# V transposed by VectorE and by a round trip through DRAM instead of by TensorE, in a convolutional attention block

## The reference, cut to what matters

```python
xn = group_norm(x)                       # x: (128, 384, 14, 14), 32 groups
q  = bn(conv1x1(xn, qw))                 # 8 heads x 32,   196 tokens
k  = bn(conv1x1(xn, kw))
v4 = bn(conv1x1(xn, vw))                 # 1024 channels = 8 heads x 128
vl = bn(depthwise_conv3x3(v4))
attn = q @ k.T * 32**-0.5 + bias         # (8, 196, 196) for each image
attn = mix_heads(attn, th1)
attn = softmax(attn)
attn = mix_heads(attn, th2)
o = relu(attn @ v + vl)
out = x + bn(conv1x1(o, pw))
```

## Time and profile before

| what | value |
|---|---|
| time, median of 3 | 4813.96 us (4813.76 to 4814.5) |
| the profiled execution, its own time | 4811.84 us |
| its span, first to last instruction | 4810.0 us |
| TensorE busy | 4779.1 us, 99% |
| VectorE busy | 4175.9 us, 87% |
| ScalarE busy | 3251.4 us, 68% |
| GpSimd busy | 988.6 us, 21% |
| DMA queue 1 | 119.93 MB, 7.4% of 16 engines |
| mean granted TensorE clock | 0.998 |
| one pair in the steady state | 74.50 us |

### The profile page before, as it was taken

One profiled execution on the slowest core, in us unless ns is written; L12 is line 12 of the kernel. 1 busy time (PEld: TensorE's weight loads), 2 busy tenths in 40 slices (PEclk: granted clock), 3 DMA queues, 4 the chain that ended last, 5 costly groups with the idle time before them and its releaser, 6 DMA issues.

```text
span 4810.0 us, 111468 instructions
## 1 busy us (share of the span) xinstructions
PE 4779.1 (99%) x35842; PEld 4760.2 (99%) x35842; DVE 4175.9 (87%) x10897; ACT 3251.4 (68%) x8005; POOL 988.6 (21%) x1093
## 2 busy tenths in 40 slices
PE   7999999999999999999999999999999999999999
PEld 7999999999999999999999999999999999999999
DVE  8888888889888898888888988889888888898887
ACT  6666666666667666667666666766666766666665
POOL 3212212121121221221212212122121221221211
PEclk9999999999999999999999999999999999999999
DMA  1000000000000000000000000000000000000000
GB/s 57 26 20 30 19 26 30 15 30 25 20 30 15 30 25 20 30 15 30 30 15 30 25 20 30 15 30 25 20 30 15 30 29 16 30 21 24 30 15 26
DMA packets 55148, 120.23 MB, mean 25 GB/s; under 512 B 3650, under 2 KB 5842, under 8 KB 55124
## 3 DMA queue, kind: packets, MB, share of 16 engines
q1 hardware_dynamic: 55124, 119.93, 7.4%
HBM read 81.38 MB, written 38.54 MB: 25 GB/s over the span
## 4 chain that ended last, share of the span: by engine, by line
PE 98%; DVE 1%; issue 0%; DMA 0%; ACT 0%; SPq 0%; DVEq 0%
PE psA L250 43%; PE psA L399 14%; PE psL L250 12%; PE psM L250 10%; PE psM L377 8%; PE psL L377 6%; PE psM L367 2%; PE psL L367 2%; DVE psC L620 1%; PE psA L268 0%; PE psA L263 0%; DMA qa<-in_wqkv 0%; DVE probs L675 0%; DVE x_lo L601 0%; DVE q_lo L650 0%
## 5 line engine op out<-in xcount | busy, mean ns | idle before, releaser
L620 DVE SCALAR_TENSOR_TENSOR psC<-vpad,par,psC 128x406 f32<-128x406 f32 x3072 | 1808.7, 637 | 0.0
L498 ACT ACTIVATE probs<-probs,nmax 112x196 f32<-112x196 f32 x1792 | 799.0, 449 | 649.0 <-DVE nmax L675 641.8
L250 PE MATMUL psA<-x_hi,w_lo 128*128 128x392 f32 x2304 | 795.0, 345 | 8.5 <-DVE x_lo L601 8.5
L250 PE MATMUL psA<-x_lo,w_hi 128*128 128x392 f32 x2304 | 788.9, 342 | 0.0
L250 PE MATMUL psA<-x_hi,w_hi 128*128 128x392 f32 x2304 | 788.1, 342 | 0.0
L399 PE MATMUL psA<-qa,shared 105*128 105x196 f32 x4096 | 693.9, 330 | 3.0 <-DVE shared L719 3.0
L399 PEld LDWEIGHTS psA<-qa,shared 105*128 105x128 f32 x4096 | 680.2, 191 | 3.3 <-DVE shared L719 3.3
L650 DVE SCALAR_TENSOR_TENSOR q_lo<-q,th,q_hi 128x392 fp32r<-128x392 f32 x1024 | 604.4, 621 | 34.6 <-ACT q_hi L442 27.6
L719 DVE TENSOR_TENSOR shared<-psA,shared 128x392 f32<-128x392 f32 x512 | 290.1, 567 | 366.5 <-PE psA L399 366.5
L442 ACT ACTIVATE q_hi<-q,th 128x392 fp32r<-128x392 f32 x1024 | 582.0, 620 | 6.0
L434 ACT ACTIVATE o_hi<-shared 128x392 fp32r<-128x392 f32 x512 | 271.5, 530 | 457.6 <-DVE shared L719 457.6
(11 more groups left out here) (85 smaller groups left out, 10500.0 us busy)
## 6 DMA issues: line engine op xcount, KB each, us to landing
xs<-in_x SPq DMA_DIRECT2D x64, 588.0 KB, 3.8
shared<-in_x SPq DMA_DIRECT2D x64, 588.0 KB, 3.8
out<-shared SPq DMA_DIRECT2D x63, 588.0 KB, 3.0
qa<-in_wqkv SPq DMA_DIRECT2D x3, 768.0 KB, 6.7
stage_wp<-in_wp SPq DMA_DIRECT2D x1, 1536.0 KB, 9.9
out<-shared SPq DMA_DIRECT2D x3, 196.0 KB, 2.0
shared<-in_abx SPq DMA_DIRECT2D x1, 165.4 KB
par<-in_par SPq DMA_DIRECT2D x1, 70.5 KB
```

The source lines that it names most:

```text
L250: last = nc.tensor.matmul(dst, w, r, start=(begin and n == 0), stop=(end and n == 2))
L498: nc.scalar.activation(row, row, ACT.Exp, bias=nmax[:, img, b:b + 1], scale=-1.0, accum_out=rowsum[:, img, b:b + 1]).then_inc(s_exp, 1)
L620: nc.vector.scalar_tensor_tensor(a if tap == 7 else sums, src, taps[:, c, TAPS[tap]:TAPS[tap] + 1], a if tap == 0 else sums, MUL, ADD).the ...
```

## The change

TensorE's transposes of V, their eight uses of the banks and the identity matrix go. In their place:

- VectorE transposes V in blocks of 32x32, in two instructions (`turn`), four channel tiles of both images each, 4 x 2 x 7 blocks, so 1,792 elements on each of 128 partitions. The result goes into `turned`, a part of the tensor that will later hold the probabilities. `turn(0)` stands after the first six convolutions, `turn(1)` after three more turns of one `mixed_low` and one convolution; the last five `mixed_low` now come together, and the six convolutions after them.
- SyncE writes the blocks to a DRAM tensor `by_key` with the pixel as its row (`turned_out`, eight DMAs: two images, four groups of 32 partitions, each DMA 32 x 7 pieces of 1 KB), restores a row of ones in the probabilities (`ones_in`), and once all logits of the pair are made reads by_key back with pixels on partitions (`keys_in`, four DMAs of 112 rows of 4 KB, into `raw`, which lies over parts of qa and of q, k_hi and k).
- ScalarE copies from `raw` to `vt`, 105x1024 elements four times (`head_major`), after mixing uses 1, 3, 10 and 13, since the channels arrive ordered by group of 32 first and channel tile second.
- VectorE waits before the scores of use 5 until the eight writes are complete, since the scores overwrite `turned`. TensorE waits for the ones before the mixing.
- k_hi and k_lo are placed so that q, k_hi and k lie next to each other.

```diff
@@ SyncE
+            def turned_out(t):
+                sp.wait_ge(s_turned, 2 * t + 2)
+                for img in range(2):
+                    for a in range(QUADS):
+                        sp.dma_start(by_key[img].rearrange("(b r) (a n) -> r a b n", r=BLK, a=QUADS)[:, a, :, :],
+                                     turned[a * BLK:(a + 1) * BLK, img, :, :, :].rearrange("p b c n -> p b (c n)")
+                                     ).then_inc(s_vt_out, 16)
+            def ones_in(t):
+                sp.wait_ge(s_vt_out, OUTS * (t + 1))
+                sp.dma_start(probs[HP:HP + 1, :, :, :].rearrange("p i b n -> p (i b n)")[:, TURNED_AT:],
+                             A["ones"]).then_inc(s_ones_in, 16)
+            def keys_in(t):
+                sp.wait_ge(s_logit_mm, 14 * (t + 1))
+                for img in range(2):
+                    for jc in range(2):
+                        sp.dma_start(raw[img][0:ROWS, jc, :],
+                                     by_key[img, jc * HALF:jc * HALF + ROWS, :]).then_inc(s_raw[img], 16)
             def step(t, first, last):
                 ...
                     load_x(t + 1)
+                turned_out(t)
+                ones_in(t)
+                keys_in(t)
                 if not first:
                     store(t)
                 residual(t + 1)
@@ TensorE
-                for use in range(22):
-                    img, (what, n) = use // 11, USES[use % 11]
-                    bank_free(use)
-                    if what == "vt":
-                        jc, cg = divmod(n, 2)
-                        for c in range(4):
-                            at_ = PITCH + 1 + img * PITCH * PITCH + jc * HALF
-                            mm = nc.tensor.transpose(mix_bank(use)[:, c * P:(c + 1) * P],
-                                                     vpad[:, 4 * cg + c, at_:at_ + HALF], ident[:, :])
-                        mm.then_inc(s_vt_mm, 1)
+                pe.wait_ge(s_ones_in, 16 * (t + 1))
+                for use, (img, n) in enumerate(USES):      # USES: 2 images x 7
                     if use < 4:
                         pe.wait_ge(s_score, 28 * t + 22 + 2 * use)
                     else:
+                        pe.wait_ge(s_mix_sb, 14 * t + use - 3)
                     ...
                 for img in range(2):
-                    pe.wait_ge(s_vt_sb, 8 * t + 4 * img + 4)
+                    pe.wait_ge(s_vt_sb, 4 * t + 2 * img + 2)
@@ ScalarE
+            def head_major(t, img, jc):
+                act.wait_ge(s_raw[img], 32 * (t + 1))
+                nc.scalar.copy(vt[0:HALF, img, jc, :].rearrange("p (c a n) -> p c a n", c=VT, a=QUADS),
+                               raw[img][0:HALF, jc, :].rearrange("p (a c n) -> p c a n", a=QUADS, c=VT)
+                               ).then_inc(s_vt_sb, 1)
+                COPIES = {1: (0, 0), 3: (0, 1), 10: (1, 0), 13: (1, 1)}
+                for use, (img, n) in enumerate(USES):
+                    act.wait_ge(s_mix_mm, 14 * t + use + 1)
+                    if use == 7:
+                        act.wait_ge(s_vt_sb, 4 * t + 2)
+                    ...  (copy of the bank to attn)
+                    if use in COPIES:
+                        head_major(t, *COPIES[use])
+                    if use == 6 and not last:
+                        act.wait_ge(s_v_mm, VT * (t + 1))
+                        x_high(t + 1)
@@ VectorE
+                def turn(half):
+                    c0 = half * (VT // 2)
+                    dve.wait_ge(s_v_sb, VT * t + c0 + VT // 2)
+                    src = vpad[:, c0:c0 + VT // 2, PITCH + 1:PITCH + 1 + 2 * PITCH * PITCH].rearrange(
+                        "p c (i n) -> p c i n", i=2)[:, :, :, 0:BLOCKS * BLK]
+                    nc.vector.transpose(turned[:, :, :, c0:c0 + VT // 2, :].rearrange("p i b c n -> p c (i b) n"),
+                                        src).then_inc(s_turned, 1)
                 mixed_low(8)
                 convs(6)
-                for _ in range(8):
+                turn(0)
+                for _ in range(3):
                     mixed_low(1)
                     convs(1)
-                convs(1)
+                turn(1)
+                mixed_low(5)
+                convs(6)
                 ...
                 for n in range(RES):
+                    if n == TURNED_ROW // 2:       # 5
+                        dve.wait_ge(s_vt_out, OUTS * (t + 1))
                     wait_alone(dve, s_logit_mm, 14 * t + n + 1)
```

More of the change, by code:

```diff
@@ L19 @@
 HALF = RES // 2 * PITCH
+ROWS = 112
+BLK = 32
+BLOCKS = 7
+QUADS = P // BLK
+PART = VT * BLK
+TURNED = 2 * BLOCKS * PART
+TURNED_AT = 2 * RES * 2 * HALF - TURNED
+TURNED_ROW = TURNED_AT // (2 * HALF)
 HR = P // KD
@@ L173, in mixed @@
                     q[:, kt, :].rearrange("p (b i) -> p b i", i=RES))
-        USES = [("vt", 0), ("mix", 0), ("vt", 1), ("mix", 1), ("vt", 2), ("mix", 2), ("vt", 3), ("mix", 3),
-                ("mix", 4), ("mix", 5), ("mix", 6)]
+        USES = [(img, n) for img in range(2) for n in range(7)]
         def logit_bank(n):
@@ new lines, in step @@
+                    else:
+                        pe.wait_ge(s_mix_sb, 14 * t + use - 3)
+                    pe.wait_ge(s_exp, 28 * t + 14 * img + 2 * n + 2)
+                    pe.wait_ge(s_mixw, 8 * t + 4 * img + group(2 * n + 1) + 1)
+                    bank = mix_bank(use)[:, 0:4 * HP].rearrange("p (j g b i) -> p j g b i", j=2, g=NH, b=2)
+                    for jc in range(2):
+                        for b in range(2):
+                            mm = nc.tensor.matmul(bank[:, jc, :, b, :],
+                                                  probs[0:HP + 1, img, 2 * n + b, jc * HALF:(jc + 1) * HALF],
+                                                  mixw[0:HP + 1, img, 2 * n + b, :].rearrange("p (g i) -> p g i", g=NH),
+                                                  start=True, stop=True)
@@ L382, in step @@
+                    mm.then_inc(s_mix_mm, 1)
                 if first:
@@ L502, in step @@
                         conv_centre(t, CENTRES[n])
[L503 to L514, removed]
-                        nc.scalar.copy(attn[:, img, :, :, 2 * n * RES:(2 * n + 2) * RES], src).then_inc(s_mix_sb, 1)
-                    if use == 16 and not last:
+                COPIES = {1: (0, 0), 3: (0, 1), 10: (1, 0), 13: (1, 1)}
+                for use, (img, n) in enumerate(USES):
+                    act.wait_ge(s_mix_mm, 14 * t + use + 1)
+                    if use == 0 and not first:
+                        act.wait_ge(s_av_mm, 8 * t)
+                    if use == 7:
+                        act.wait_ge(s_vt_sb, 4 * t + 2)
+                    src = mix_bank(use)[:, 0:4 * HP].rearrange("p (j g m) -> p j g m", j=2, g=NH)
+                    nc.scalar.copy(attn[:, img, :, :, 2 * n * RES:(2 * n + 2) * RES], src).then_inc(s_mix_sb, 1)
+                    if use in COPIES:
+                        head_major(t, *COPIES[use])
+                    if use == 6 and not last:
                         act.wait_ge(s_v_mm, VT * (t + 1))
@@ L657, in step @@
                 convs(6)
-                for _ in range(8):
+                if not first:
+                    dve.wait_ge(s_mix_mm, 14 * t)
+                turn(0)
+                for _ in range(3):
                     mixed_low(1)
                     convs(1)
-                convs(1)
+                turn(1)
+                mixed_low(5)
+                convs(6)
                 if not first:
```

46 lines of the change are left out of this document (16 added, 30 removed).

## The result

The changed kernel takes 4881.93 us (median of 4 runs, 4881.75 to 4884.25), the kernel before 4813.9 us beside it: a ratio of 1.0142, 95% interval 1.0126 to 1.0158. I forecast 4841 us. The direction is right and the time lies in the stated range, but the loss is 68 us where I had 27. The profiled execution has a span of 4880.2 us.

The account below looks back on a forecast made before the run. VectorE was to become the bound at 74.4 us a pair, just under TensorE's old 74.50: 4813.96 - 2.5 + 30 us for clock falls = 4841.5, say 4841 us, 0.56% slower; range 4804 to 4940.

Parts of the forecast that it names:

- TensorE's saving: Mixing stage: eight uses of V transposes go, 3.5 us a pair, so the stage falls from 14.26 to 10.7 us.
- T: Start of VectorE's first addition of the AV products in a pair; the logits were forecast at T + 36.6.
- The transposes: VectorE: two added transposes of 128x1792 elements, 1.93 us each, 3.85 us a pair.
- VectorE as the bound, using up 3.29 us of slack: VectorE's chain: the added transposes use up its idle time before the first addition, giving pairs of 74.4 us.
- the recurring 2.46 us: VectorE's wait before the pair's first convolution, for a chain starting after the additions; said to return however late VectorE is.
- ScalarE and the transfers: V's DRAM writes and reads hidden, image 0's reads landing in 4.7 us; head_major copies 1.0 us each, just covered.
- The stall: TensorE stands still 2.4 us a pair before logits use 4, waiting for the scores of use 0.
- six pairs in ten, at 0.8 us, 0.48 us a pair: Clock falls to 1.2 GHz after TensorE's stop: assumed frequency and net price, 30 us over 63 pairs.
- the 1.3 us that I counted: TensorE's spare time per pair against VectorE's chain, said to cover 1.3 us of a clock fall's cost.
- my 0.6 to 2.0 us: Forecast net cost of a clock fall in a pair that has one.
- the time without falls: Whole program with the clock staying up: 2.5 us less, about 4811 us; as a rival, no change, chance 0.25.
- The first pair: VectorE has no slack there already, so the transposes' 3.85 us were added in full.

Follow-up runs that it names:

- fill24: Changed kernel plus 24 harmless 120-column matmuls filling TensorE's stop after logits use 2; 4802.22 us, 0.9976 of the kernel before.
- split_proj: Changed kernel with half of the third projection tile (12 matmuls) moved from behind the logits into the stop after logits use 2; 4803.3 us, 0.9979.
- defer3: Changed kernel with 3 of the 8 convolutions before the second projection's addition moved behind the scores; 4862.35 us, 1.0101.
- tiny_turn: Changed kernel with each VectorE transpose cut to a single 32x32 block, all transfers and ScalarE copies kept; 4654.24 us, 0.9670.
- sums3: Changed kernel with the group sums asked for after logits use 3 instead of use 2, cutting the stop in two; 4853.06 us, 1.0083.
- add_turn: Kernel before, plus VectorE's two transposes and their wait for the mixing, TensorE keeping its own transposes of V; 5110.62 us, 1.0617.
- pool4b: Changed kernel with 4 low parts of scaled queries on GpSimd, only 784 ones loaded behind the logits, ahead of V's reads; 4717.76 us, 0.9800.
- defer7: Changed kernel with 7 of the 8 convolutions before the second projection's addition moved behind the scores; 5151.01 us, 1.0702.
- pool4: Changed kernel with 4 low parts of scaled queries on GpSimd and the whole row of ones loaded behind the logits; 5152.46 us, 1.0701.
- pool6: Changed kernel with 6 low parts of scaled queries on GpSimd and the whole row of ones loaded behind the logits; 5068.19 us, 1.0529.

## Why the loss was two and a half times the forecast

**TensorE's saving: right.** The mixing runs from 2426.75 to 2437.48, 10.73 us (10.7 forecast), the logits begin at T + 36.7 (36.6), and the pair that TensorE alone sets is 71.2 us (71.0).

**The transposes: right.** 1.96 us each (1.93). The Trainium skill, "Vector Engine (DVE) Microarchitecture Reference" (The reshape front-end), by which the estimate was 1.87 us plus start-up, agrees with this row.

**VectorE as the bound, using up 3.29 us of slack: right.** Forecast 74.4 us without falls of the clock; fill24, split_proj and the better pairs of defer3 give 74.22 to 74.24. The first convolution stands 20.46 us behind the first addition (20.4 worked out), the recurring 2.46 us stayed. Without falls the change would have gained 12 us (fill24), where I had 2.5.

**ScalarE and the transfers: right.** head_major took 1.05 us (1.0), image 0's keys landed in 4.2 us (4.7), and tiny_turn shows the whole trip hidden.

**The stall: right size, wrong owner.** 2.68 us where I had 2.4. I followed the bank of psL from use 4 to the scores and overlooked the bank of psA: the group sums wait for the projection's evacuation, which VectorE reaches just before the scores. sums3 shows that the wait I named is next in line, 0.81 us.

**The term that failed: "six pairs in ten, at 0.8 us, 0.48 us a pair".** Both of its factors were too small. The runs show 62 pairs of 62, at 75.33 - 74.22 = 1.1 us in the ordinary pair and 2.6 us in every eighth: 1.29 us a pair, 80 us in all where I had 30. A fall in every pair at my 0.8 us would be 50 us; the other 30 are its price. The fall itself costs 1.7 us of TensorE (defer3, add_turn), of which the spare time behind the logits covers 0.6 us, not the 1.3 us that I counted: VectorE is held up already within the scores (waits up to 0.38 us for late logits in the ordinary pair and none in fill24; from the first convolution to the next addition 54.9 us instead of 53.8), and what VectorE loses there is lost, though TensorE has time to spare later. The mean price lay inside my 0.6 to 2.0 us, the 2.6 us of every eighth pair outside; the frequency was a guess with two stops and two falls behind it. It was no absurd one: in defer3 a stop that recurs at the same place is harmless in every other pair. By luck the miss is not larger still: the time without falls had come out 9 us too high (a gain of 2.5 us for 12), and that took back part of the 50 us that this term was short. Why every eighth pair pays double isn't settled.

The Trainium skill, "TensorE: Matmul & The Clock Gate" (Why this matters for your kernels), asks for a longer gap than this before the clock falls. The measurements disagree with it: 2.68 us were enough in every pair, 1.51 and 0.81 us close together in 60 of 62, 1.9 us in about half.

**The first pair: too low.** 5.95 us until the first addition where I had 3.85. Even tiny_turn is 3.7 us later there than the kernel before (93.23 for 89.54), so not all of it is the transposes. The traces show the rest. Two convolution taps that read `vpad` and the accumulator, both in SBUF, meet GpSimd's first-pair work on the low part of the projection weights and on x:

```profile
76.71 11.20 DVE L643 SCALAR_TENSOR_TENSOR psC<-vpad,par,shared 128x406 f32<-128x406 f32 x2
...
77.22 6.72 POOL L822 TENSOR_TENSOR wp_lo<-stage_wp,wp_hi 128x3072 fp32r<-128x3072 f32 x1
83.90 2.68 POOL L782 TENSOR_TENSOR x_lo<-xs,x_hi 128x1176 fp32r<-128x1176 f32 x1
```

The first of them takes 10.3 us, in the kernel before 7.7. The eight taps of this kind take 15.4 us in the first pair where they took 12.4: 3.0 us, beside 3.9 of the transposes, while the first convolution begins 0.7 us earlier.

## What to carry to other kernels

Work taken from the bounding engine and given to the second one counts only up to the second engine's real slack, and its lateness comes back to the first engine as a stop. Ask then two things: which of *all* the waits on the late engine comes first, small instructions with a bank of their own included, and what TensorE does after the stop; the fall after a stop of two or three microseconds cost 1.7 us more of TensorE and 0.8 to 1.7 us of the ordinary pair, so filling the stop with useless matmuls gained 80 us, and with half a projection tile as much. Taking the second engine's load down (here to GpSimd, 20% busy) is worth far more than either: 4.2% below the kernel before.

## What was not expected of the hardware

- Single stops of 1.03 to 1.10 us (defer3, split_proj) and 1.37 us (pool4b) brought no fall in the steady state, one of 2.68 us always did, and 1.87 and 1.90 us in neighbouring pairs of one program went either way. Stops of 1.51 and 0.81 us close together brought one in 60 pairs of 62.
- The filling matmuls of 120 columns start 0.11 us apart where logits matmuls of 196 columns start 0.098 apart. Their weight loads stand 0.11 and 0.098 us apart as well, with 128 columns of weights in the one and 112 in the other, so the load may be what sets the pace; no run separates it from the width.
- A VectorE instruction with two inputs in SBUF slows down beside GpSimd: 657 to 1,004 ns for a convolution tap (defer7), 618 to 686 ns for a low part (pool4b). Split within one run, the taps of defer7 that overlap a GpSimd instruction take 1,208 ns and the others 645, the low parts of pool4b 810 and 623; in the first pair a tap lasted 10.3 us. The Trainium skill, "Trainium Architecture — The Big Picture" (What this means for kernel authors), says that these two engines share a port pair under an exclusive lock. The rows agree that the one holds up the other, for as long as 10.3 us; the lock itself they don't show.
- A transfer of 23.5 KB, needed at once, came late enough for 5 us of waiting because four of 448 KB had been issued ahead of it (pool4, pool6); its own packet took 1.1 us.
